# One hybrid block on one core: shorter norms in the first phase, fourteen identity products early on TensorE, and the calls of all engines in a new order

## What is computed

```python
x = x + mamba(layernorm(x))      # the part that the change touches
x = x + moe(layernorm(x))
x = x + rwkv(layernorm(x))
x = x + moe(layernorm(x))
```

```python
q = rope(x @ Wq.T)                                     # 128 features
h = q * rsqrt(mean(q*q) + 1e-5) * norm_pre_w
z, xBC, dt = split(h @ W_zxbcdt.T)                     # 256, 512, 4
xBC = silu(causal_conv_4_taps(xBC) + conv_b)           # x_ssm 256, B 128, C 128
y = ssd(x_ssm, softplus(dt + dt_bias), A, B, C) + D * x_ssm
y = rmsnorm(y * silu(z), norm_gated_w)
out = y @ W_out.T + q
```

## Time and profile before

| | us |
|---|---|
| three runs | 495.67, 495.52, 494.61 |
| their median | 495.52 |
| the profiled execution | 494.99 |
| its span, first to last instruction | 493.3 |
| end of the first phase in it | 126.5 |
| the rest of it | 366.8 |

### The profile page before, as it was taken

The page is one execution under the profiler, slowest core; times in us unless marked ns, Lnnn a source line. Parts: engine busy times, 40 slices in busy tenths (PEclk is TensorE's granted clock), DMA queues, the critical chain, the costliest instruction groups (busy, mean ns, idle before and its releaser), DMA issues.

```text
span 493.3 us, 10648 instructions
## 1 busy us (share of the span) xinstructions
PE 471.2 (96%) x3706; PEld 326.2 (66%) x3706; DVE 390.1 (79%) x1044; ACT 355.8 (72%) x687; POOL 365.6 (74%) x448
## 2 busy tenths in 40 slices
PE   7898999999799999998999999999999989999996
PEld 7575789988466666666565756576666756666664
DVE  5899999678766868899878897978887868467765
ACT  1699999774857867955896858694877566858652
POOL 4655886986485776799878978987989586456662
PEclk9999999999999999999999999999999999999999
DMA  7000222000200000000000000000000000000000
GB/s 268 23 2 1 66 64 66 0 2 2 72 1 0 2 1 2 3 0 1 2 1 1 1 2 1 0 2 2 2 18 5 2 1 23 2 1 1 23 1 23
DMA packets 7061, 8.51 MB, mean 17 GB/s; under 512 B 608, under 2 KB 5216, under 8 KB 7008
## 3 DMA queue, kind: packets, MB, share of 16 engines
q1 hardware_dynamic: 7008, 7.83, 4.9%
HBM read 6.78 MB, written 1.05 MB: 16 GB/s over the span
## 4 chain that ended last, share of the span: by engine, by line
PE 54%; DVE 9%; POOL 5%; ACT 4%; issue 2%; DVEq 0%; ACTq 0%; POOLq 0%
PE bank L1577 9%; PE bank L1581 9%; PE bank L1578 9%; PE bank L1604 5%; PE bank L1606 5%; PE bank L1605 5%; PE bank L1721 3%; PE bank L1704 2%; PE bank L1647 2%; PE bank L1648 2%; POOL b_hc L2250 1%; DVE x L1965 1%; DVE b_hid L1939 1%; PE bank L1611 1%; PE bank L1632 1%
## 5 line engine op out<-in xcount | busy, mean ns | idle before, releaser
L2188 POOL TENSOR_TENSOR b_hid_lo<-b_hid,b_hid_hi 128x512 f16<-128x512 f32 x143 | 166.9, 1179 | 51.4 <-ACT b_hid_hi L1783 49.3
L1939 DVE SCALAR_TENSOR_TENSOR b_hid<-bank,b_silu 128x512 f32<-128x512 f32 x144 | 97.7, 688 | 55.4 <-ACT b_silu L1776 38.1
L1776 ACT ACTIVATE b_silu<-bank 128x512 f32<-128x512 f32 x144 | 85.8, 596 | 57.7 <-PE bank L1581 56.6
L1577 PE MATMUL bank<-x_hi,wsplit 128*128 128x512 f16 x284 | 107.7, 379 | 2.4 <-ACT b_silu L1776 1.9
L1581 PE MATMUL bank<-x_lo,wsplit 128*128 128x512 f16 x284 | 107.6, 379 | 0.0
L1578 PE MATMUL bank<-x_hi,wsplit 128*128 128x512 f16 x284 | 107.6, 379 | 0.0
L1783 ACT CAST b_hid_hi<-b_hid 128x512 f16<-128x512 f32 x144 | 88.2, 612 | 22.2 <-DVE b_hid L1939 21.9
L1604 PE MATMUL bank<-wsplit,b_hid_hi 128*128 128x128 f16 x576 | 100.2, 219 | 2.5 <-POOL b_hid_lo L2188 1.7
L1605 PE MATMUL bank<-wsplit,b_hid_hi 128*128 128x128 f16 x576 | 100.1, 219 | 0.0
L1606 PE MATMUL bank<-wsplit,b_hid_lo 128*128 128x128 f16 x576 | 100.1, 219 | 0.0
L1965 DVE SCALAR_TENSOR_TENSOR x<-bank,b_w_branch,x 128x128 f32<-128x128 f32 x256 | 71.5, 341 | 12.1 <-PE bank L1606 11.9
(11 more groups left out here) (247 smaller groups left out, 947.9 us busy)
## 6 DMA issues: line engine op xcount, KB each, us to landing
moe_raw<-in_moe SPq DMA_DIRECT2D x9, 384.0 KB, 3.7
x<-in_x SPq DMA_DIRECT2D x4, 256.0 KB, 4.4
out<-x SPq DMA_DIRECT2D x3, 256.0 KB, 2.3
rope<-in_rope SPq DMA_DIRECT2D x1, 512.0 KB, 5.9
wzx<-in_wzx SPq DMA_DIRECT2D x1, 386.0 KB, 6.3
b_w_rkvo<-in_w_rkvo SPq DMA_DIRECT2D x1, 256.0 KB, 2.6
b_w_fk<-in_w_fk SPq DMA_DIRECT2D x1, 256.0 KB, 2.9
b_w_fv<-in_w_fv SPq DMA_DIRECT2D x1, 256.0 KB, 3.3
```

Of the source, the lines that this page charges most:

```text
L1577: nc.tensor.matmul(dst, hi, x_hi[:, q % 2, :], start=True, stop=False)
L1776: nc.scalar.activation(silu[:, 2 * (u % 2) + blk, :], gate_ps[blk][:, :], ACT.Silu, scale=GU_UNSCALE).then_inc(silu_ready, 1)
L1939: nc.vector.scalar_tensor_tensor(hid[:, 2 * (u % 2) + blk, :], up_ps[blk][:, :], GU_UNSCALE * H_SCALE, silu[:, 2 * (u % 2) + blk, :], ALU. ...
L2188: nc.gpsimd.tensor_tensor(hid_lo[:, slot, :], hid[:, 2 * (u % 2) + blk, :], hid_hi[:, slot, :], ALU.subtract).then_inc(lo_ready, 1)
```

## The change

The norms lose small POOL steps. `normalise` takes mean and rstd themselves (subtract, multiply), so -mean * rstd isn't made for it; the same goes for `apply_norm`, and `rsqrt_out` raises its semaphore after the power. The divisions by 128 and 256 of the two RMS norms become the factors P ** 0.5 in the scaling step and INNER ** 0.5 in `w_gated`; their eps becomes one more column of q and g, filled once, that Square sums along. Three memsets are added for it. `warm_up` goes from 22 to 12 products, and 14 single ones, `keep_warm`, are put between the steps of PE's list up to the first `turn_tok`. The lists of all four engines are written in another order; apart from `keep_warm` the calls in them are the same.

```diff
+                for k in range(2):
+                    nc.gpsimd.memset(g[:, k, INNER:INNER + 1], (INNER * EPS) ** 0.5)
+                nc.gpsimd.memset(q[:, :, P:P + 1], (P * EPS) ** 0.5)
...
             def rsqrt_var(s):
-                link(nc.gpsimd.tensor_tensor(rstd[:, a:b], veps[:, a:b], core.mhalf[:, a:b], ALU.pow))
-                link(nc.gpsimd.tensor_tensor(nbias[:, a:b], mv[:, a:b, 0], rstd[:, a:b], ALU.mult))
-                nc.gpsimd.tensor_scalar(nbias[:, a:b], nbias[:, a:b], -1.0, 0.0, ALU.mult,
-                                        ALU.add).then_inc(rstd_ready, 1)
+                nc.gpsimd.tensor_tensor(rstd[:, a:b], veps[:, a:b], core.mhalf[:, a:b],
+                                        ALU.pow).then_inc(rstd_ready, 1)
...
             def rms_q(s):
-                link(nc.gpsimd.tensor_scalar(ssq[:, a:b], ssq[:, a:b], 1.0 / P, EPS, ALU.mult, ALU.add))
...
-                    nc.gpsimd.tensor_scalar(norm[:, i, :], q[:, i, :], rms[:, i:i + 1], 0.0,
-                                            ALU.mult, ALU.add).then_inc(h_ready, 1)
+                    nc.gpsimd.tensor_scalar(norm[:, i, :], q[:, i, 0:P], rms[:, i:i + 1], P ** 0.5,
+                                            ALU.mult, ALU.mult).then_inc(h_ready, 1)
...
             def rms_g(n):
-                link(nc.gpsimd.tensor_scalar(ms2[:, i:i + 1], ssq2[:, i:i + 1], 1.0 / INNER, EPS, ALU.mult, ALU.add))
-                nc.gpsimd.tensor_tensor(rms2[:, i:i + 1], ms2[:, i:i + 1], core.mhalf[:, 0:1],
+                nc.gpsimd.tensor_tensor(rms2[:, i:i + 1], ssq2[:, i:i + 1], core.mhalf[:, 0:1],
...
-                    nc.vector.tensor_scalar(norm[:, i, :], x[:, i, :], rstd[:, i:i + 1], nbias[:, i:i + 1],
-                                            ALU.mult, ALU.add).then_inc(xn_ready, 1)
+                    nc.vector.tensor_scalar(norm[:, i, :], x[:, i, :], mv[:, i, 0:1], rstd[:, i:i + 1],
+                                            ALU.subtract, ALU.mult).then_inc(xn_ready, 1)
...
+            def keep_warm(k):
+                nc.tensor.matmul(tok_ps[:, 0:P], core.ident[:], core.ident[:], start=True, stop=True)
```

More of the change, by code:

```diff
@@ L899, in _ @@
             square_q(15)
+            tap0(1, 0)
+            copy_hT(2)
+            conv_silu(0, 0, 2)
+            tap0(1, 1)
+            conv_silu(0, 2, 4)
+            copy_hT(3)
             tap0(1, 2)
+            conv_silu(1, 0, 2)
+            dt_exp()
+            tap0(1, 3)
+            dt_log()
             tok_out(0)
-            conv_silu(1, 0, 2)
+            tap0(2, 0)
+            z_silu(4)
+            conv_silu(1, 2, 4)
+            tap0(2, 1)
             tok_out(1)
-            tap0(1, 3)
@@ L905, in _ @@
-            z_silu(4)
+            segments(0)
+            tap0(2, 2)
             tok_out(2)
-            copy_hT(3)
-            tap0(2, 0)
             z_silu(5)
-            conv_silu(1, 2, 4)
-            dt_exp()
-            tok_out(3)
-            dt_log()
-            tap0(2, 1)
-            tok_out(4)
-            segments(0)
             decay_exp()
             seg_exp(0)
-            tap0(2, 2)
+            split_high(2)
+            tok_out(3)
             segments(2)
             seg_exp(1)
-            split_high(2)
+            tap0(2, 3)
@@ L923, in _ @@
+            tok_out(4)
+            split_high(3)
+            seg_exp(2)
             tok_out(5)
-            tap0(2, 3)
-            seg_exp(2)
-            split_high(3)
-            tok_out(6)
+            segments(4)
             seg_exp(3)
             z_silu(6)
+            tap0(3, 0)
+            tok_out(6)
+            copy_gT(0)
+            z_silu(7)
             square_g(0)
-            tap0(3, 0)
-            z_silu(7)
-            segments(4)
-            copy_gT(0)
+            conv_silu(2, 0, 4)
@@ L1239, in _ @@
+            keep_warm(12)
+            keep_warm(13)
             turn_tok(0)
+            project_in(1, 3)
+            project_in(2, 0)
             project_z(4)
             turn_tok(1)
-            project_in(1, 3)
+            project_in(2, 1)
+            project_z(5)
+            products(0)
+            project_in(2, 2)
             turn_tok(2)
-            turn_h(3)
-            project_in(2, 0)
-            project_z(5)
-            project_dt(3)
-            project_in(2, 1)
-            turn_tok(3)
@@ L1264, in _ @@
[L1264 removed]
+            turn_tok(5)
+            products(4)
+            turn_g(0)
             seg_sums(3)
             within(1)
[L1267 removed]
             project_in(3, 1)
+            seg_sums(4)
+            turn_tok(6)
+            products(5)
             project_z(7)
[L1270 to L1273 removed]
             within(2)
             project_out(0)
[L1276 removed]
+            add_state(0)
@@ L1277, in _ @@
+            project_in(3, 2)
             add_state(1)
+            turn_tok(7)
             carry(2)
-            seg_sums(4)
-            turn_tok(8)
-            project_in(3, 2)
+            turn_g(1)
+            products(6)
             add_state(2)
-            turn_g(1)
+            seg_sums(5)
             carry(3)
             within(3)
+            turn_tok(8)
+            add_state(3)
+            seg_sums(6)
             project_out(1)
             turn_tok(9)
-            seg_sums(5)
+            carry(4)
@@ L1304, in _ @@
             project_out(3)
-            seg_sums(8)
-            products(7)
             seg_sums(9)
+            carry(6)
+            products(8)
+            within(6)
+            add_state(8)
             turn_g(4)
-            add_state(5)
-            carry(6)
+            seg_sums(10)
+            carry(7)
             turn_tok(12)
             project_out(4)
-            within(6)
-            products(8)
+            products(9)
+            within(7)
+            products(10)
+            turn_tok(13)
@@ L1346, in _ @@
             within(11)
-            seg_sums(13)
+            project_out(9)
+            turn_tok(15)
+            within(12)
+            products(14)
+            turn_g(10)
             carry(12)
-            project_out(9)
-            within(12)
-            seg_sums(14)
             turn_first()
-            turn_g(10)
+            project_out(10)
             add_state(12)
-            products(14)
             products(15)
+            seg_sums(15)
+            turn_g(11)
+            within(13)
```

500 lines of the change are left out of this document (247 added, 253 removed).

## The result

The changed kernel takes 490.85 us (median of four runs, 490.74 to 491.06); the kernel before, beside it, 495.45. The ratio is 0.9912, 95% interval 0.9897 to 0.9927: 4.6 us faster, where 3.0 was forecast. The profiled execution took 490.91 with a span of 489.2. One of the ten executions of `orders_only` took 605.91 us at a mean granted clock of 0.754 and isn't in its ratio.

The account below looks back on a forecast made before the run. Bounds: ScalarE and VectorE together at 20 to 50 us, PE at 64 to 110, latencies at the first phase's end. Gains 2.2 + 0 + 0.8 = 3.0 us take the median from 495.52 to 492.5; range 490.0 to 495.2.

Parts of the forecast that it names:

- The second phase, 0: From the meeting of the engines at 126.5 us to the end: untouched, 0, plus or minus 0.3 us.
- Opening, lead 1.7 at `turn_x` and spent by 13.5: 0 to 20 us: shorter warm-up brings turn_x(0) from 10.0 to about 7.8; first turn_q at 13.5, no lead in time.
- The nine and the five identity products, 0: keep_warm on PE in opening and convolution: nine cost nothing, covered by 2 us; five fall in waits, uncovered 1.1.
- One more table load: ScalarE, 20 to 50 us: one extra load between dt_log and decay_exp, 1.28 us without a drain, inside the walk.
- 20 to 64 us, a lead of 2.2: Convolution and up to 64 us: steps come earlier, less the work put off behind them; taken as 2.2 us.
- 64 to 110 us, 0, because PE had 0.34 us free: Stretch with PE full: lead neither grows nor shrinks much, 0; bounds a loss of 2.2 to a gain of 1.3.
- 110 us to the end, 0.8: Last stretch of first phase: seg_sums(15) ahead of two within ends ScalarE's 3.6 us wait; gain 0 to 3.6, taken 0.8.
- POOL's relief, covered by PE, 0: 64 to 110 us: sixteen rms_g each lose a 281 ns step, 4.5 us in all; PE covers it.
- The sum, 3.0: Whole kernel: 2.2 + 0 + 0.8 = 3.0 us faster, median 495.52 to 492.5.
- The full relief: Rival, 0.15: POOL sets PE's pace at 90 to 110 us and the tail packs, 2.2 + 1.3 + 1.6 = 5.1: 490.4.
- The lost lead: Rival, 0.14: late POOL or DVE steps idle PE in the full 46 us; gain only 0 to 0.9: 495.1.
- The slow side: Rival, 0.09: PE stops at 5.9 us, short weight loads come late and the query's products stretch: 497.5.

Follow-up runs that it names:

- orders_only: Kernel before with its old norms but all the new lists, warm_up(12) and the fourteen keep_warm among them; 493.56 us, ratio 0.9973.
- after_no_keep: Changed kernel without the fourteen keep_warm, warm_up(12) kept; 491.49 us, ratio 0.9936.
- head_old: Kernel before with the shorter norms, old lists up to finish_dt with warm_up(22), then the new order; 492.51 us, ratio 0.9957.
- tail_new_norms: Kernel before with the shorter norms, old lists up to turn_first with warm_up(22), then the new order; 493.51 us, ratio 0.9972.
- norms_only: Kernel before with the shorter norms alone: old lists on all engines, warm_up(22), no keep_warm; 495.04 us, ratio 1.0000.
- after_long_rms_g: Changed kernel with one more small POOL step and its wait put back in rms_g, result the same; 492.41 us, ratio 0.9952.
- head_new: Kernel before with old norms, new lists up to finish_dt (warm_up(12) and keep_warm), then the old order; 496.18 us, ratio 1.0033.
- after_wq_late: Changed kernel with the DMA of wq issued behind the second piece of x instead of the first; 490.80 us, ratio 0.9919.
- after_old_tail: Changed kernel up to turn_first, then what is left in the old order; 492.96 us, ratio 0.9966.
- after_no_warm: Changed kernel without warm_up and without any of the fourteen keep_warm; 493.10 us, ratio 0.9956.
- tail_new: Kernel before with old norms, old lists up to turn_first (warm_up(22), no keep_warm), then the new order; 493.27 us, ratio 0.9964.

## Why the prediction was right, point by point

- **The second phase, 0.** Right: 366.75 against 366.80.
- **Opening, lead 1.7 at `turn_x` and spent by 13.5.** Right in kind, with an error in the rate. "7 of them per us" doesn't follow from loads of 333 ns: the records start 0.213 us apart while the loads are long, 4.7 per us, so the 24 end at 7.87 and not at 5.9, and PE has no pause of 2 us before `turn_x`. `turn_x` came near 7.8 all the same. The norm came earlier than I had it, for a DMA that landed earlier, and `turn_q` stands 5.8 to 5.9 us behind the first norm in all profiles with the new opening (12.64 here).
- **The nine and the five identity products, 0.** Right by the profile of `after_no_keep`; two of its six executions had more of the lower clock (last section).
- **One more table load.** There are eleven instead of ten, each 1.28 us, with no drain ahead: in the changed kernel the load at 65.80 follows `conv_silu`, which ends at 63.88 + 1.90 = 65.78.
- **20 to 64 us, a lead of 2.2.** Right in sign and too large: 0.9 to 1.7 by the rows, 1.7 by `head_old` against the changed kernel, the shorter warm-up counted in. The terms missed are the wait of 0.90 for POOL's `add_q` and waits for `tap0`, where I had ScalarE come in time: 0.3 each at three later blocks and 0.83 at `taps(3,0)`.
- **64 to 110 us, 0, because PE had 0.34 us free.** This step was wrong in its ground. A busy share of overlapping records can't show a hole shorter than the overlap: by spacing PE had 2 us without work there before and 1.2 after. `head_old` against `tail_new_norms` gives the middle 1.0.
- **110 us to the end, 0.8, "near what PE has".** Too small, by the same error. PE had 3.6 us without work behind `turn_first`, not 1.16, and the new order leaves 1.1. The profiles give the tail 1.0 to 1.5, the medians 1.5 to 2.1, and `seg_exp(15)` lost its wait as forecast (109.72 instead of 118.11).
- **POOL's relief, covered by PE, 0.** Half right. Under the old lists it is worth nothing (`norms_only`); under the new ones 1.6 by the medians and 0.8 by the profile (`after_long_rms_g`). It was covered by holes that the new order closes.
- **The sum, 3.0.** That it lies within the range owes something to luck: the lead of 2.2 was too large, middle and tail were too small by 0.8 to 1.0 and 0.2 to 1.3, and these errors offset each other in part. I had no term for the clock or for the warm-up's varying length, which are in the 4.6.
- **Rivals.** The full relief, 490.4, was the nearest to what came: its terms 1.3 and 1.6 for middle and tail are near the 0.8 to 1.0 and 1.0 to 2.1 measured, and its reason, POOL setting the pace at 96 us and in the last stretch, was at work. The lost lead was in part true of a new head under old lists (`head_new`). The slow side didn't come about: the first `project_q` has loads of 191 ns at 10.5 us. Its ground, a stop of PE at 5.9 for 2 us, was the error in the rate.

## What to carry to other kernels

A busy share near 100% of an engine whose records overlap doesn't mean that it is full: add up the spacing of its groups instead, and see how much is left. A step that hides behind a bound is worth nothing only until an order closes the holes; norms and order together gave 4.6 us by the medians, where the norms alone gave 0 and the order alone 1.7. An order worked out for a whole phase isn't the sum of its parts: a good head in front of an old middle was slower than no change, while a good tail worked with anything ahead of it. And when a kernel's executions fall into groups, a median counts how often each group occurs too: compare the phase's own ends, and look whether two profiles of the same opening agree, before a difference of 1 us is given a cause.

## What the runs showed that was not expected

- **The clock falls for a few us in some executions, just behind the meeting of the engines.** The same stretch of `after_wq_late` and of the changed kernel (the clock stands last but two):

```profile
129.00:133.00 4.00, 4.00 (x19) 1.83 (x18) 2.77 (x10) 2.61 (x5) 3.50 (x4) 0.57 0.31 102
```

```profile
129.00:133.00 4.00, 4.00 (x37) 2.53 (x37) 3.44 (x12) 2.87 (x6) 3.65 (x4) 1.00 0.38 127
```

  TensorE goes to the lower of its two levels (1.2 GHz) for most of it; PE had been busy for 1.08 of the 3.00 us before. The rest of that kernel then takes 368.50 us instead of 366.75, 1.75 more. The changed kernel had the same 1.09 of 3.00 and kept its clock, so it isn't the pause alone. Four of the fourteen profiles have falls: `after_wq_late` and `after_old_tail` behind the meeting, `head_old` at 51 us, and `after_no_warm` at 41 us (0.60 over 41 to 45) and behind the meeting. The one at 41 us cost nothing that lasts: PE's steps are 1.02 us later than in the changed kernel at 18 us, 2.0 later at 45 and 1.02 again from 47 us on. The slow start and the fall behind the meeting are this kernel's loss.
- **The new tail goes with fewer falls.** A profile with one fall has a mean clock of 0.997. Of the executions of the kernel before that were timed beside the experiments 34 of 70 have it, with a median of 495.8; those at 0.999 or more have 494.7. With the new lists, 490.85 without a fall, that leaves 3.8 us of the 4.6. Of all kernels with the old tail 44 of 106 executions have 0.997, of those with the new tail 7 of 59, leaving out the two without identity products. None of the 21 of `tail_new` and `tail_new_norms` is among the 7, and two of them are of `head_old`, whose profile has its fall at 51 us. Why isn't shown, nor where the falls of executions without a profile lie.
- **Without the identity products there were falls that no other kernel had.** A mean clock of 0.993 (two falls in the one profile that shows it) stands in 2 of 6 executions of `after_no_keep` and 5 of 10 of `after_no_warm`, and in none of the 165 others, the one at 0.754 left out. The kernels with the old opening have none of the fourteen either, but 22 products at the start. So with the short warm-up the fourteen may be worth something in some executions, though nothing in the profiled one; six executions are few.
- **The kernel before varies without any fall.** Its executions at 0.999 or more run from 493.44 to 495.28. The length of the warm-up is one cause that the profiles show: 44 records in 6.70 us in `norms_only` and 7.92 in the kernel before.
- **POOL's power of one column takes 0.55 us, and up to 1.1 beside some steps of VectorE.** `rms2` of one tile in the changed kernel: 0.55 in nine of its sixteen calls, two in 1.91 beside `split_low`, and 0.84 to 1.00 in three calls that overlap `mixing`, though not in every one that does. In `after_long_rms_g` 1.14 at 121.05 beside `split_low`. The new tail puts three `split_low` in a row where the last two `rms_g` are due.
- **Landings wander.** The second piece of x is taken up between 5.22 and 6.07 us in the thirteen profiles with the DMAs in the old order; with the new head, which has no other slack before 12 us, the phase's end follows it.
